# Attention scores in four row groups over four banks that they share with the transposed probabilities, in the first phase of a transformer stack on one core

## What is computed

```python
qh, kh, vh = heads(q), heads(context), heads(context)        # 16 heads of 8
scores = einsum('bhqd,bhkd->bhqk', qh, kh) + mask            # layer 1: clipped, then masked
weights = softmax(scores, axis=-1)
ctx = einsum('bhqk,bhkd->bhqd', weights, vh)
x = x + relu(ctx @ wo_w.T + wo_b)                            # layer 0
# layer 0's feed-forward: router, 2 of 8 experts for each token, hidden 512
h = relu(einsum('td,edh->teh', xf, W1) + b1); y = einsum('teh,eho->teo', h, W2) + b2
```

## The kernel before

| engine | order within turn n |
|---|---|
| PE | scores n, work 0, transposes n-1, work 1, product n-2, transposes of `ou` n-3, work 2 |
| ACT | work 0, `ou` n-3, copy to `pt` n-1, work 1, exponentials n, work 2 |
| DVE | work 0, division n-4, mask n, maximum n, work 1, copy to `pt` n-1, work 2, work 3 |

## Time and profile before

### The profile page before, as it was taken

How to read it: one execution, slowest core, us unless ns; L and a number is a source line. 1 busy time by engine, 2 the same in 40 slices (tenths; PEclk the granted TensorE clock), 3 DMA queues, 4 the chain that set the end, 5 groups by cost and what they waited for, 6 DMA issues and landing times.

```text
span 2441.3 us, 49251 instructions
## 1 busy us (share of the span) xinstructions
PE 1941.3 (80%) x17184; PEld 1549.6 (63%) x17184; DVE 1508.2 (62%) x3920; ACT 1294.3 (53%) x4431; POOL 628.8 (26%) x626
## 2 busy tenths in 40 slices
PE   3887977878689878447788889898998887878864
PEld 2666866667577656135666667776776766666664
DVE  5886865757567788555566665655656554555442
ACT  2755554545455656435576756565665654544421
POOL 0002021311411220013233343242342423232331
PEclk9877999879899987557799999898998999999987
DMA  7002444343344200310000011122221222222253
GB/s 212 28 16 89 121 123 128 101 125 106 112 139 120 67 22 6 113 41 17 26 6 13 6 56 50 50 66 77 66 66 49 74 76 79 74 83 78 76 153 107
DMA packets 125124, 184.17 MB, mean 75 GB/s; under 512 B 10320, under 2 KB 82064, under 8 KB 124624
## 3 DMA queue, kind: packets, MB, share of 16 engines
q1 hardware_dynamic: 116688, 164.23, 22.8%
q0 software_dynamic: 8192, 16.79, 2.4%
HBM read 145.52 MB, written 35.45 MB: 74 GB/s over the span
## 4 chain that ended last, share of the span: by engine, by line
PE 34%; DVE 9%; ACT 6%; issue 6%; POOL 1%; DMA 1%; SPq 0%; DVEq 0%; ACTq 0%; POOLq 0%
PE ps L1610 6%; PE ps L1859 4%; ACT pb L1999 4%; PE ps L1838 3%; PE ps L1845 3%; PE ps L1648 3%; PE ps L1632 2%; DVE nm L2351 2%; PE ps L1639 2%; PE ps L1621 2%; PE ps L1817 2%; PE ps L1666 1%; DVE hT L2142 1%; ACT pt L2007 1%; DVE hT L2137 1%
## 5 line engine op out<-in xcount | busy, mean ns | idle before, releaser
L1999 ACT ACTIVATE pb<-ps,nm 128x128 f32<-128x128 f32 x1024 | 363.3, 377 | 264.1 <-DVE nm L2351 263.9
L2040 POOL TENSOR_TENSOR pb<-pb,rcs 128x512 f32<-128x512 f32 x256 | 266.7, 1042 | 803.8 <-DVE rcs L2340 802.3
L964 ACT ACTIVATE pb<-pb,nm 128x128 f32<-128x128 f32 x1024 | 313.0, 391 | 92.6 <-DVE nm L1187 90.3
L2351 DVE TENSOR_REDUCE nm<-ps 128x8 f32<-128x1024 f32 x128 | 156.1, 1219 | 138.3 <-PE ps L1845 71.5
L2360 DVE COPY pt<-ps 128x512 f32<-128x512 f32 x128 | 88.3, 690 | 223.0 <-PE ps L1859 223.0
L1999 ACT ACTIVATION_READ_ACCUMULATOR pb<-ps,nm 128x1 f32 x1024 | 222.0, 217 | 0.0
L1859 PE MATMUL ps<-w,pb 128*128 128x128 f32 x1024 | 173.9, 297 | 49.8 <-ACT pt L2007 42.7
L1610 PE MATMUL ps<-hT,big 128*128 128x128 f32 x960 | 151.8, 308 | 54.7 <-DVE hT L2142 44.1
L851 PE MATMUL ps<-w,pb 128*128 128x128 f32 x1024 | 168.9, 309 | 28.7 <-ACT pb L964 18.6
L1610 PEld LDWEIGHTS ps<-hT,big 128*128 128x128 f32 x960 | 135.4, 216 | 80.1 <-DVE hT L2142 58.4
L1859 PEld LDWEIGHTS ps<-w,pb 128*128 128x128 f32 x1024 | 128.2, 153 | 80.8 <-issue 68.0
(11 more groups left out here) (365 smaller groups left out, 4387.8 us busy)
## 6 DMA issues: line engine op xcount, KB each, us to landing
big<-in_we SPq DMA_DIRECT2D x92, 514.0 KB
big<-in_we SPq DMA_DIRECT2D x120, 384.0 KB
big<-sorted_in SPq DMA_DIRECT2D x8, 960.0 KB, 6.5
sorted_out<-big SPq DMA_DIRECT2D x28, 256.0 KB
sorted_in<-big SPq DMA_DIRECT2D x4, 1472.0 KB, 12.1
sorted_out<-h_all SPq DMA_DIRECT2D x16, 256.0 KB
hidden<-h_all SPq DMA_DIRECT2D x7, 512.0 KB, 2.9
h_all<-hidden SPq DMA_DIRECT2D x7, 512.0 KB, 3.9
```

What stands on the lines that cost most here:

```text
L964: m = a.activation(pb[:, n % 2, k * S:(k + 1) * S], pb[:, n % 2, k * S:(k + 1) * S], ACT.Exp, bias=nm[:, n % 2, k:k + 1])
L1999: m = a.activation(pb[:, n % 2, e * S:(e + 1) * S], ps[:, score_bank(n) + half, k * S:(k + 1) * S], ACT.Exp, bias=nm[:, n % 2, e:e + 1], a ...
L2040: g_.tensor_tensor(p4, p4, r4.unsqueeze(2).to_broadcast([P, 4, S]), ALU.mult).then_inc(n2["p_normed"], 1)
L2351: v.tensor_reduce(nm[:, n % 2, :], ps[:, bank:bank + 2, :].rearrange("p a (j k) -> p (a j) k", k=S), AX, ALU.max, negate=True).then_inc(n2 ...
```

## The change

Scores use all four row groups: for each half `c` of the heads, the four groups of 32 partitions with two heads each. A unit's eight heads are therefore others than before (`head_of`), and the division writes them to their places with a stride. The scores go to the first halves of banks 0 to 3. The transposed probabilities go to banks 0 and 1, the same ones. So scores n must wait until both copies to `pt` of unit n-2 are done, and the transposes of n-1 until the mask has read scores n. The product with the values and the transposes of `ou` move on PE to just behind the scores, work 1 moves between the two halves of the transposes, ACT copies to `pt` ahead of `ou` and takes `ou` one unit sooner, and DVE divides one unit sooner, behind the maximum. For layer 1 the clip is two instructions of 128x512 instead of one of 128x1024.

```diff
         def mask1_clip(v, out, scores, mask):
-            return v.scalar_tensor_tensor(out, scores, -100.0, mask.unsqueeze(1).to_broadcast([P, BLK, S]),
-                                          ALU.max, ALU.min)
+            for i in range(2):
+                m = v.scalar_tensor_tensor(out[:, :, i, :], scores[:, :, i, :], -100.0, mask.unsqueeze(1).to_broadcast([P, 4, S]),
+                                           ALU.max, ALU.min)
+            return m
...
                         if n:
                             pe.wait_ge(s["masked"], n)
+                        if n >= 2:
+                            pe.wait_ge(s["p_hi"], n - 1)
+                            pe.wait_ge(s["p_lo"], n - 1)
                         for k in range(BLK):
-                            i, a = divmod(k, 2)
-                            at = 32 * (2 * c + a)
-                            m = pe.matmul(ps[:, a, i * S:(i + 1) * S], qms[r][at:at + 32, i, b * S:(b + 1) * S],
-                                          keys[r][at:at + 32, b * S:(b + 1) * S], start=True, stop=True)
+                            i, a = divmod(k, 4)
+                            m = pe.matmul(ps[:, a, i * S:(i + 1) * S], qms[r][32 * a:32 * a + 32, 2 * c + i, b * S:(b + 1) * S],
+                                          keys[r][32 * a:32 * a + 32, b * S:(b + 1) * S], start=True, stop=True)
                         m.then_inc(s["scores"], 1)
-                    work(0, n)
-                    if 0 <= n - 1 < NUN:
-                        p = n - 1
-                        for k in range(BLK):
-                            if k % 4 == 0:
-                                pe.wait_ge(s["exps"], 2 * p + 1 + k // 4)
-                                if p:
-                                    pe.wait_ge(s["p_lo" if k else "p_hi"], p)
...
-                    work(1, n)
...
-                    work(2, n)
+                    work(0, n)
+                    for half in range(2):
+                        if 0 <= n - 1 < NUN:
+                            p = n - 1
+                            pe.wait_ge(s["exps"], 2 * p + 1 + half)
+                            if n < NUN:
+                                pe.wait_ge(s["masked"], n + 1)
+                            elif p:
+                                pe.wait_ge(s["p_lo" if half else "p_hi"], p)
+                            for k in range(4 * half, 4 * half + 4):
+                                m = pe.transpose(ps[:, half, (k % 4) * S:(k % 4 + 1) * S], pb[:, p % 2, k * S:(k + 1) * S],
+                                                 ident)
+                            m.then_inc(s["transposed"], 1)
+                        work(1 + half, n)
```

More of the change, by code:

```diff
@@ L571, in mask0_add @@
         def mask0_add(v, out, scores, mask):
-            return v.tensor_tensor(out, scores, mask.unsqueeze(1).to_broadcast([P, BLK, S]), ALU.add)
+            return v.tensor_tensor(out, scores, mask.unsqueeze(1).unsqueeze(1).to_broadcast([P, 4, 2, S]), ALU.add)
         def mask1_clip(v, out, scores, mask):
-            return v.scalar_tensor_tensor(out, scores, -100.0, mask.unsqueeze(1).to_broadcast([P, BLK, S]),
-                                          ALU.max, ALU.min)
+            for i in range(2):
+                m = v.scalar_tensor_tensor(out[:, :, i, :], scores[:, :, i, :], -100.0, mask.unsqueeze(1).to_broadcast([P, 4, S]),
+                                           ALU.max, ALU.min)
+            return m
         ORDER = [(layer, g) for layer in range(2) for g in range(NG)]
@@ L633, in build, with head_of @@
         s = att_a
+        def head_of(c, k):
+            return 4 * (k // 2) + 2 * c + k % 2
         ctx_rows = ctx_d.rearrange("b s d -> s b d")
@@ L958, in _ @@
                             a.wait_ge(s["pv"], p - 1)
-                        a.activation(pt[:, p % 2, 0:4 * S], ps[:, 2, :], ACT.Copy).then_inc(s["p_hi"], 1)
+                        a.activation(pt[:, p % 2, 0:4 * S], ps[:, 0, :], ACT.Copy).then_inc(s["p_hi"], 1)
+                    if 0 <= n - 2 < NUN:
+                        p = n - 2
+                        a.wait_ge(s["pv"], p + 1)
+                        if p:
+                            a.wait_ge(s["normed"], p)
+                        a.activation(ou[:, :], ps[:, 4, 0:2 * S], ACT.Copy).then_inc(s["o_read"], 1)
                     work(1, n)
@@ L1187, in _ @@
                         v.tensor_reduce(nm[:, n % 2, :], buf, AX, ALU.max, negate=True).then_inc(s["maxed"], 1)
+                    if 0 <= n - 3 < NUN:
+                        p = n - 3
+                        j, u = divmod(p, NU)
+                        b, c = divmod(u, 2)
+                        turned = ps[:, 4, 2 * P:4 * P].rearrange("p (k d) -> p k d", d=32)
+                        v.wait_ge(s["o_turned"], p + 1)
+                        v.reciprocal(rc[:, :], turned[:, :, DH]).then_inc(s["o_recip"], 1)
+                        v.wait_ge(s["o_recip"], p + 1)
+                        if u == 0 and j >= 2:
+                            v.wait_ge(s["oT_psum"], j - 1)
+                        v.tensor_tensor(os_[j % 2][:, b, :].rearrange("p (a c i d) -> p c a i d", a=4, c=2, i=2)[:, c],
+                                        turned[:, :, 0:DH].rearrange("p (a i) d -> p a i d", i=2),
+                                        rc[:, :].rearrange("p (a i) -> p a i", i=2).unsqueeze(3)
+                                        .to_broadcast([P, 4, 2, DH]), ALU.mult).then_inc(s["normed"], 1)
                     work(1, n)
@@ L1193, in _ @@
                             v.wait_ge(s["pv"], p - 1)
[L1194 removed]
+                        v.tensor_copy(pt[:, p % 2, 4 * S:8 * S], ps[:, 1, :]).then_inc(s["p_lo"], 1)
                     work(2, n)
```

29 lines of the change are left out of this document (3 added, 26 removed).

## The result

| | before | after |
|---|---|---|
| median of 4 runs each, us | 2443.18 | 2532.69 |
| ratio, 95% interval | | 1.0369 [1.0352, 1.0386] |
| span of the profiled execution | 2441.3 | 2528.2 |
| PE busy over the span | 1941.3 (80%) | 1905.3 (75%) |
| DVE busy | 1508.2 (62%) | 1520.6 (60%) |

The change made the kernel 3.7% slower, some 90 us. I had forecast slower, but by 28 us, and the time lies 3 us above the range. All of it is in the first phase. The start of the maximum shows it (L1187 before, L1183 after): from unit 0 to unit 127 it takes 924.9 us before and 1017.6 after, 92.7 more. Of these 21 fall on units 0 to 32, 52 on units 32 to 104, and 19 on units 104 to 127. The last 1441 us of both executions have the same PE busy time within 7 us. Over the stretch of the 128 maxima PE is idle 285 us for 163 before, though its busy time fell from 762 to 733 us.

A forecast was written before the change was run, and what follows sets the result against it. No single bound in the first phase: PE paces some units, DVE others. Terms +7 (plain units), +4 (clip), +21 (DVE-heavy tiled units), +19 (hidden tiles), -23 (PE-paced units) sum to +28 on 2443.1: 2470 us, range 2400 to 2530.

The forecast's parts named there:

- the clip in two: Layer 1's clip on DVE: two instructions take 1.28 instead of 1.22 us, +4 us over 64 units.
- the scores' block: PE's 16 score records at full clock: 28 ns a record with four row groups, block 0.69 us, 0.47 less.
- The second rival: Scores on PE: four row groups are no faster than two, 2487 to 2503 us; chance 0.12.
- the plain unit: Units without other DVE work, full clock: mask to mask grows from 3.36 to about 4.2 to 4.4 us.
- the ring, and the wait for `ou`: PE in the first phase: new waits on DVE's mask and copy total over 80 us; its 30.4 us wait for `ou` goes.
- the hidden tile at place 0: Eight units where DVE evaluates a hidden tile before the mask: PE idles 2.4 us in each, +19 us.
- the walk through units 73 to 77: Tiled stretch with DVE about 90% busy, masks followed: 2.55 us more in four units, 0.64 a unit.
- the term of +21 us: About 33 of the 68 tiled units, with over 1.5 us of DVE work between copy and mask: +21 us.
- what work 1 costs between the halves: Between the transpose halves: rank matmuls 1.9 us in the tiled stretch; 10 hidden tiles at place 1 nothing, +4 at most.
- the 60 units without tiles: Seven units with no other DVE work lose 1.0 us each, +7 us; no change at the lower clock.
- the saving: The other 35 or so tiled units, paced by PE, gain 0.65 us each, -23 us, including the vanished `ou` wait.
- The third rival: More idle PE brings more stretches at the lower clock: 30 more such units add 48 us, 2518 us; chance 0.11.

The follow-up runs named there:

- order_w1b: Changed kernel with two row groups, own banks, no new waits on copies or mask, and work 1 behind both transpose halves: 1.0116 of the kernel before.
- ring_w1b: order_w1b plus both waits, scores n for both copies of unit n-2 and transposes n-1 for the mask of unit n: 1.0382 of the kernel before.
- work1_behind: Changed kernel with work 1 moved back behind both halves of the transposes: 1.0200 of the kernel before.
- transposes_wait: order_w1b plus only one wait, transposes n-1 for the mask of unit n: 1.0202 of the kernel before.

## Why the prediction was right and wrong

What failed are two terms that had next to no price. The place of work 1 between the halves was priced only by the rank matmuls in the walk and at "+4 at most" for the tiles; it costs 41 us. The rest of the new order was put at nothing, or at a gain through the sooner `ou`; it costs 28 us. The ring and the four groups, the terms that had a price, came to +21 us for +28, but by two misses that cancel: the ring cost more than its busy times said, and the groups gave more. Step by step from the kernel before:

| step | forecast, us | measured, us |
|---|---|---|
| rest of the order (order_w1b) | 0, and a gain by a sooner `ou` inside the -23 | +28 |
| ring (ring_w1b) | +7 + 21 + 19 | +65 |
| four row groups, the clip in two (work1_behind) | -23 + 4 | -44 |
| work 1 between the halves (the change) | only the rank matmuls, inside the +21 | +41 |
| sum | +28 | +90 |

The steps depend on each other: work 1 costs 0.9 to 1.0% with two groups and 1.7% with four, and the ring 6.9% under the old order. The last two steps also join runs of different chips. So it is one path and not a set of constants. That the ring and the groups together came out near their sum is luck.

**Right: the scores' block.** I had 0.69 us and 28 ns a record; measured are 0.73 and (0.73 - 0.27)/15 = 31 ns. The Trainium skill (TensorEngine Tiling (Array Packing), Key Properties) has tiles load weights and multiply independently, and the trace agrees: four groups run at 31 ns where two ran at 59. The scores' weight loads last 187 ns each at the median, as before, and not the 107 ns worked out in the prediction; 16 of either length, one after the other, would be more than the block's 0.73 us, so the loads of four groups overlap. The second rival, no gain from four groups, is excluded. PE's busy time for the scores fell from 171 to 112 us in the phase.

**Right: the plain unit.** 4.38 us, forecast 4.2 to 4.4.

**Right: the clip in two.** 1.29 us for 1.22, as forecast.

**Right: the ring, and the wait for `ou`.** New waits on mask and copy were forecast at over 80 us together and are 187, more than twice that; the wait for `ou` went.

**Right: the hidden tile at place 0.** In each of the 8 units PE is idle 2.4 to 2.6 us in front of the transposes, 20 us together, as priced (+19). What these 20 us are worth in time no run isolates.

**Wrong: the walk through units 73 to 77, and with it the term of +21 us.** The masks of that stretch in the changed kernel:

```profile
641.13 1.29 DVE L577 SCALAR_TENSOR_TENSOR pb<-ps,mask1i 128x512 f32<-128x512 f32 x2
...
649.93 1.28 DVE L577 SCALAR_TENSOR_TENSOR pb<-ps,mask1i 128x512 f32<-128x512 f32 x2
...
660.14 1.29 DVE L577 SCALAR_TENSOR_TENSOR pb<-ps,mask1i 128x512 f32<-128x512 f32 x2
...
670.06 1.29 DVE L577 SCALAR_TENSOR_TENSOR pb<-ps,mask1i 128x512 f32<-128x512 f32 x2
...
678.09 1.28 DVE L577 SCALAR_TENSOR_TENSOR pb<-ps,mask1i 128x512 f32<-128x512 f32 x2
```

They start 8.80, 19.01, 28.93 and 36.96 us from the first, where I had 7.95, 18.1, 27.15 and 33.9: +5.6 us over the 31.35 of the earlier trace rows instead of +2.55. The steps missed by 0.85, 0.06, 0.87 and 1.28 us. PE's timeline says what I left out:

```profile
645.25 1.12 PE L812 MATMUL ps<-w,big 8*128 8x128 f32 x8 [0.72 <-ACT ctxT L926]
...
664.07 1.16 PE L742 MATMUL ps<-h_all,big 128*128 128x128 f32 x8 [1.00 <-ACT h_all L898]
...
671.49 0.74 PE L883 MATMUL ps<-w,pb 128*128 128x128 f32 x4 [2.46 <-DVE pb L577]
672.02 1.92 PE L750 MATMUL ps<-big,hT 128*128 128x128 f32 x8
673.73 1.06 PE L883 MATMUL ps<-w,pb 128*128 128x128 f32 x4
```

I had put every block of work into the ring at its busy time at full clock. But PE waits 0.72 and 1.00 us for ACT in front of two of them, in the first and the third step, and the second of these waits is for an item that PE used to reach later than ACT (in turn 75 before, PE began L736 at 606.22 us without a wait). In the fourth step PE was without a matmul for 2.46 us, the granted clock behind that was 0.50, the lower level (672 to 674 us), and the output tile took 1.92 us for 1.06. Each of these delays reached the next mask. That a chain with slack would have absorbed them is my reading.

**Wrong: what work 1 costs between the halves.** Its place cost 41 us, 36 of them (1.5 of 1.7%) by projections, transposes and router steps. In the forecast only the rank matmuls stood there, 2 us at a time; in the trace all these steps together take 48 us of PE's time between the halves and 21 us of waits in front of them, and DVE's copy stands behind both. At place 1 I had said "+4 at most", for the tiles; for these that was nearly right.

**Wrong: the 60 units without tiles.** I had +7, and no change at the lower clock. Units 0 to 32 and 104 to 127 lost 40 us, 21 of them at a clock of 0.80 for 0.81. The turns with layer norms and projections, which I took to be hidden, have them in the ring, as unit 109 above; how much of the 40 us is theirs isn't isolated.

**Partly wrong: the saving.** PE-paced units were to gain 23 us. Four groups are worth 27 us in the changed kernel, near that figure, and 44 with work 1 out of the ring. But I had also counted a gain from the sooner `ou`. That wait went, and yet the new order costs 28 us (1.2%) where nothing else is changed. Which part of it costs is open.

**The lower clock.** The third rival is in part true: the clock is 0.84 for 0.90 in the tiled window, and 0.74 for 0.82 in units 104 to 127. It isn't the whole: units 0 to 32 lost 21 us at nearly the same clock, and transposes_wait was 2.0% slower at a mean clock of 0.899 over the execution, where the kernel before had 0.894 on the same chip. How many of the 90 us are the clock's I can't say: no run changes the clock without the waits, since no bank is left for matmuls that would only keep PE busy.

## What to carry to other kernels

Sharing a buffer between two steps of neighbouring units makes a ring of semaphores, and a ring can cost more than the busy times in it: here 65 us, and 41 more for work placed inside it, where busy times at full clock gave 47. Price each block in the ring with what another engine must finish before it, and move out of it all that needn't be there. But don't price by the length of one link: the way from the copy to the scores was made shorter in two ways, and nothing was gained. And a faster block is worth less than its time where the engine then waits: here 59 us less of matmul time for the scores brought 27 to 44.

## What was not expected of the hardware

Issuing the scores in pairs (groups 0 and 1, then 2 and 3) ran as fast as in turn over all four: 0.74 us for 16 records against 0.73. At the lower clock the block takes 1.24 us, against 2.08 with two groups, the same ratio within 6%. And the same kernel ran at 2351 us on one chip and 2453 on another, a difference larger than the change's.
